# The first loads and the last three tiles of an adaptive feed-forward kernel, in another order

## What is computed

```python
q_emb = relu(cond @ W3 + b3)                              # 32 x 512
v = (64 * x + x.sum(axis=1, keepdims=True)) * q_emb[:, None, :]
h0 = relu(v @ W2 + b2)                                    # 2048 rows x 512
h = square(relu(h0 @ ternary(W_fc).T))                    # 2048 x 2048
hn = h * rsqrt(mean(h * h, axis=-1) + eps)
out = x + hn @ ternary(W_proj).T                          # 2048 x 512
```

## Time and profile before

| | us |
|---|---|
| median of 3 runs | 311.33 |
| lowest and highest of them | 311.01 and 311.59 |
| the profiled execution | 311.1 |
| its span, from the first to the last record | 309.3 |
| PE busy in it | 304.5 |
| ACT busy | 191.2 |
| DVE busy | 187.2 |
| POOL busy | 115.0 |

### The profile page before, as it was taken

One profiled execution on the slowest core, in us unless ns is written; L12 is line 12 of the kernel. 1 busy time (PEld: TensorE's weight loads), 2 busy tenths in 40 slices (PEclk: granted clock), 3 DMA queues, 4 the chain that ended last, 5 costly groups with the idle time before them and its releaser, 6 DMA issues.

```text
span 309.3 us, 3792 instructions
## 1 busy us (share of the span) xinstructions
PE 304.5 (98%) x1279; PEld 232.6 (75%) x1279; DVE 187.2 (61%) x311; ACT 191.2 (62%) x282; POOL 115.0 (37%) x106
## 2 busy tenths in 40 slices
PE   8999999999999999999999999999999999999995
PEld 8654545447888888888888888888888888888883
DVE  0689999994888778886257335942223484222245
ACT  1773566796999599976746444455554445555540
POOL 1044676646433323335333331353333314333330
PEclk9999999999999999999999999999999999999999
DMA  7993743362654044113005200340000034000003
GB/s 259 366 312 120 223 117 105 102 139 65 196 147 102 1 102 37 34 34 68 2 0 170 103 0 1 136 139 0 0 0 2 0 136 138 0 0 0 2 2 137
DMA packets 30293, 27.03 MB, mean 87 GB/s; under 512 B 17689, under 2 KB 19777, under 8 KB 30273
## 3 DMA queue, kind: packets, MB, share of 16 engines
q1 hardware_dynamic: 29936, 26.22, 29.3%
q10 hardware_dynamic: 336, 0.56, 0.5%
HBM read 18.39 MB, written 4.19 MB: 73 GB/s over the span
## 4 chain that ended last, share of the span: by engine, by line
PE 98%; DVE 0%; issue 0%; DVEq 0%
PE ps_out L382 38%; PE ps_acc L370 38%; PE ps_acc L354 18%; PE ps_out L341 2%; PE ps_out L332 1%; PE ps_acc L425 1%; PE ps_x L442 1%; PE ps_x L416 0%; DVE x_sb L587 0%; DVE x_t L517 0%; PE ps_x L422 0%; PE ps_acc L429 0%; PE ps_acc L437 0%; DVEq L504 0%
## 5 line engine op out<-in xcount | busy, mean ns | idle before, releaser
L265 POOL TENSOR_TENSOR wv_sb<-wv_sb 128x512 f32<-128x512 f32 x55 | 71.8, 1306 | 122.6 <-DVE y_lo L532 115.5
L370 PE MATMUL ps_acc<-h_hi,w_t 128*128 128x512 f32 x256 | 100.0, 391 | 0.0
L382 PE MATMUL ps_out<-w_t,y_hi 128*128 128x512 f32 x256 | 100.0, 391 | 0.0
L382 PE MATMUL ps_out<-w_t,y_lo 128*128 128x512 f32 x256 | 99.7, 389 | 0.0
L370 PE MATMUL ps_acc<-h_lo,w_t 128*128 128x512 f32 x256 | 99.6, 389 | 0.0
L530 DVE CAST y_hi<-x_t 128x512 fp32r<-128x512 f32 x64 | 32.6, 510 | 87.5 <-PE ps_out L382 73.0
L679 ACT ACTIVATE x_t<-ps_acc 128x512 f32<-128x512 f32 x64 | 37.9, 592 | 62.5 <-PE ps_acc L370 62.5
L354 PE MATMUL ps_acc<-x_t,wv_sb 128*128 128x512 f32 x128 | 56.3, 593 | 0.3 <-DVE x_t L517 0.3
L370 PEld LDWEIGHTS ps_acc<-h_lo,w_t 128*128 128x128 f32 x256 | 48.1, 188 | 10.2 <-issue 0.2
L370 PEld LDWEIGHTS ps_acc<-h_hi,w_t 128*128 128x128 f32 x256 | 48.0, 188 | 10.2 <-issue 0.2
L382 PEld LDWEIGHTS ps_out<-w_t,y_lo 128*128 128x128 f32 x256 | 48.1, 188 | 9.9
(11 more groups left out here) (60 smaller groups left out, 172.7 us busy)
## 6 DMA issues: line engine op xcount, KB each, us to landing
x_sb<-in_x_dram SPq DMA_DIRECT2D x5, 1024.0 KB, 5.4
raw<-in_L_ffn_W_fc_dram SPq DMA_DIRECT2D x8, 512.0 KB, 6.3
raw<-in_L_ffn_W_proj_dram SPq DMA_DIRECT2D x8, 512.0 KB, 4.2
out_dram<-x_sb SPq DMA_DIRECT2D x16, 256.0 KB, 2.1
x_odd<-in_x_dram SPq DMA_DIRECT2D x2, 1024.0 KB, 7.8
x_sb<-in_x_dram SPq DMA_DIRECT2D x4, 256.0 KB, 4.2
wv_sb<-in_L_cond_W_dram SPq DMA_DIRECT2D x4, 256.0 KB, 7.6
x_t<-in_L_cond_W_dram ACTq DMA_DIRECT2D x1, 512.0 KB, 4.7
```

Of the source, the lines that this page charges most:

```text
L265: engine.tensor_tensor(acc, acc, y_sq[:, v % SQ_RING, :], ALU.add).then_inc(sq_added, 1)
L370: last = pe.matmul(ps_acc[:, (UNITS + v) % ACC_RING, :], w_t[:, j, k * P:(k + 1) * P], part[:, k, g * BANK:(g + 1) * BANK], start=(k == 0 ...
L382: last = pe.matmul(ps_out[:, t, :], part[:, v % RING, t * P:(t + 1) * P], w, start=(opens(v) and part is y_hi), stop=(closes(v) and part i ...
```

## The change

Six edits go together.

1. The load of the query's weight moves from ACT's queue to SP's, right behind the four row tiles of x.
2. PE's first work becomes the sums of x: cond's turn, the biases' turn and the query's products leave their places. The turns stand behind row tile 2, the products behind row tile 3. One semaphore serves both turns, so cond's turned copy waits for the biases too.
3. Six matmuls on zeros stand at the start in place of seven.
4. The last three tiles (61, 62, 63) are projected row tile by row tile. sum_squares stands inside row tile 0, between tiles 62 and 63.
5. y_hi and y_lo of tiles 62 and 63 lie in the place of h0_hi and h0_lo of group 0, so their split waits for no projection. DVE adds tile 63's squares between the rounding and the remainder of tile 63, not ahead of tile 62.
6. The last output row tile is finished and written in two halves of 256 columns.

```diff
@@ constants
-WARM_UP = 7
+WARM_UP = 6
...
+    BY_ROWS = TILES - 3
+    SPARE = TILES - 2
...
+    def pieces(n):
+        whole = [(t, slice(0, BANK)) for t in range(TT)]
+        if n < GROUPS - 1:
+            return whole
+        return whole[:-1] + [(TT - 1, slice(0, BANK // 2)), (TT - 1, slice(BANK // 2, BANK))]
...
+        def y_part(whole, spare, v):
+            return whole[:, v % RING, :] if v < SPARE else spare[:, v - SPARE, 0:BANK]
+
+        def y_hi_of(v):
+            return y_part(y_hi, h0_hi, v)
+
+        def y_lo_of(v):
+            return y_part(y_lo, h0_lo, v)
@@ SP
             for t in range(TT):
                 sp.dma_start(x_sb[:, t, :], x_rows[0, :, t, :]).then_inc(x0_loaded[t], 16)
+            sp.dma_start(wq_sb[:], w_q.rearrange("(k p) d -> p k d", p=P)).then_inc(wq_loaded, 16)
             load_wv(0)
...
-                for t in range(TT):
+                for i, (t, cols) in enumerate(pieces(n)):
                     if n == 1:
-                        sp.wait_ge(merged, t + 1)
+                        sp.wait_ge(merged, i + 1)
                     else:
-                        sp.wait_ge(finished, TT * (n + 1) + t + 1)
-                    sp.dma_start(out_rows[STRETCHES[n + 1][0], t], x_res[:, t, :]).then_inc(stored, 16)
+                        sp.wait_ge(finished, TT * (n + 1) + i + 1)
+                    sp.dma_start(out_rows[STRETCHES[n + 1][0], t][:, cols], x_res[:, t, cols]).then_inc(stored, 16)
...
-            sp.wait_ge(stored, 16 * TT * GROUPS)
+            sp.wait_ge(stored, 16 * (TT * GROUPS + 1))
@@ PE
-            def project_last_two():
-
-                pe.wait_ge(split, TILES - 1)
-                project_tile(TILES - 2, 0)
-                project_tile(TILES - 2, 1)
-                pe.wait_ge(split, TILES)
-                project_tile(TILES - 1, 0)
-                project_tile(TILES - 1, 1)
-                for t in range(2, TT):
-                    project_tile(TILES - 2, t)
-                    project_tile(TILES - 1, t)
+            def project_by_rows():
+
+                for t in range(TT):
+                    for v in range(BY_ROWS, TILES):
+                        if t == 0:
+                            if v == TILES - 1:
+                                sum_squares(GROUPS)
+                            pe.wait_ge(split, v + 1)
+                        project_tile(v, t)
...
-            pe.wait_ge(ident_ready, 1)
-            pe.wait_ge(cond_loaded, 16)
-            for k in range(KQ):
-                last = pe.transpose(ps_acc[:, 0, k * BATCHES:(k + 1) * BATCHES], cond_sb[:, k * P:(k + 1) * P],
-                                    ident_f[0:BATCHES, 0:BATCHES])
-            last.then_inc(condt_done, 1)
             pe.wait_ge(consts_ready, 1)
             for t in range(TT):
-                if t == TT // 2:
-                    pe.wait_ge(condt_ready, 1)
-                    pe.wait_ge(biases_loaded, 32)
-                    pe.transpose(ps_acc[:, 0, KQ * BATCHES:KQ * BATCHES + 2 * KD], bias_sb,
-                                 ident_f[0:2 * KD, 0:2 * KD]).then_inc(biases_turned, 1)
-                    pe.wait_ge(wq_loaded, 16)
-                    for m in range(KD):
-                        for k in range(KQ):
-                            last = pe.matmul(ps_x[:, m * BATCHES:(m + 1) * BATCHES], wq_sb[:, k, m * P:(m + 1) * P],
-                                             cond_t[:, k, :], start=(k == 0), stop=(k == KQ - 1))
-                    last.then_inc(q_done, 1)
                 pe.wait_ge(x0_loaded[t], 16)
                 for k in range(KD):
                     last = sum_x_block(0, t, k)
                     if t == TT - 1:
                         last.then_inc(xt_done, 1)
+                if t == TT - 2:
+
+                    pe.wait_ge(ident_ready, 1)
+                    pe.wait_ge(cond_loaded, 16)
+                    for k in range(KQ):
+                        pe.transpose(ps_acc[:, 0, k * BATCHES:(k + 1) * BATCHES], cond_sb[:, k * P:(k + 1) * P],
+                                     ident_f[0:BATCHES, 0:BATCHES])
+                    pe.wait_ge(biases_loaded, 32)
+                    pe.transpose(ps_acc[:, 0, KQ * BATCHES:KQ * BATCHES + 2 * KD], bias_sb,
+                                 ident_f[0:2 * KD, 0:2 * KD]).then_inc(condt_done, 1)
+            pe.wait_ge(condt_ready, 1)
+            pe.wait_ge(wq_loaded, 16)
+            for m in range(KD):
+                for k in range(KQ):
+                    last = pe.matmul(ps_x[:, m * BATCHES:(m + 1) * BATCHES], wq_sb[:, k, m * P:(m + 1) * P],
+                                     cond_t[:, k, :], start=(k == 0), stop=(k == KQ - 1))
+            last.then_inc(q_done, 1)
...
             project(TILES - 4)
-            project(TILES - 3)
-            sum_squares(GROUPS)
-            project_last_two()
+            project_by_rows()
@@ DVE
             def split_y(v):
                 dve.wait_ge(y_ready, v + 1)
-                if v >= RING:
+                if RING <= v < SPARE:
                     dve.wait_ge(*projected_at(v - RING))
-                dve.tensor_copy(y_hi[:, v % RING, :], y[:, v % RING, :]).then_inc(hi_done, 1)
+                dve.tensor_copy(y_hi_of(v), y[:, v % RING, :]).then_inc(hi_done, 1)
+                if v == TILES - 1:
+                    add_squares(dve, v)
                 dve.wait_ge(hi_done, v + 1)
-                dve.tensor_tensor(y_lo[:, v % RING, :], y[:, v % RING, :], y_hi[:, v % RING, :], ALU.subtract).then_inc(split, 1)
+                dve.tensor_tensor(y_lo_of(v), y[:, v % RING, :], y_hi_of(v), ALU.subtract).then_inc(split, 1)
...
-                for t in range(TT):
+                for t, cols in pieces(r - 1):
                     dve.wait_ge(tile_summed, TT * r + t + 1)
-                    dve.scalar_tensor_tensor(out=x_res[:, t, :], in0=ps_out[:, t, :], scalar=rstd[:, t:t + 1],
-                                             in1=x_res[:, t, :], op0=ALU.mult, op1=ALU.add).then_inc(finished, 1)
+                    dve.scalar_tensor_tensor(out=x_res[:, t, cols], in0=ps_out[:, t, cols], scalar=rstd[:, t:t + 1],
+                                             in1=x_res[:, t, cols], op0=ALU.mult, op1=ALU.add).then_inc(finished, 1)
...
-            dve.wait_ge(biases_turned, 1)
...
-                if v == TILES - 2:
-                    add_squares(dve, TILES - 1)
                 split_y(v)
@@ ACT
             act.dma_start(cond_sb, cond).then_inc(cond_loaded, 16)
-            act.dma_start(wq_sb[:], w_q.rearrange("(k p) d -> p k d", p=P)).then_inc(wq_loaded, 16)
```

More of the change, by code:

```diff
@@ L188, in adaln_ffn @@
         biases_loaded = sem("biases_loaded")
-        biases_turned = sem("biases_turned")
         biases_ready = sem("biases_ready")
@@ L380, in project_tile @@
                     wait(pe, finished, TT * (r - 1) + t + 1)
-                for part in (y_hi, y_lo):
-                    last = pe.matmul(ps_out[:, t, :], part[:, v % RING, t * P:(t + 1) * P], w,
-                                     start=(opens(v) and part is y_hi), stop=(closes(v) and part is y_lo))
+                for part in (y_hi_of, y_lo_of):
+                    last = pe.matmul(ps_out[:, t, :], part(v)[:, t * P:(t + 1) * P], w,
+                                     start=(opens(v) and part is y_hi_of), stop=(closes(v) and part is y_lo_of))
                 if closes(v):
```

## The result

The changed kernel takes 313.17 us (median of 6 runs, 312.40 to 313.47), the kernel before 311.17 (median of 6, 310.69 to 311.59). The ratio is 1.0068, with a 95% interval of 1.0057 to 1.0079: slower by 2.0 us, clear of the 0.2% that a measurement can tell. The forecast was 311.9, no measurable change, with a range up to 312.7.

What follows compares the result with a forecast made beforehand. The prediction took PE to bound the kernel, with 304.5 of 309.3 us busy. Its terms, 0.73 + 0.44 + 0.10 - 0.75 = +0.52 us on 311.33, gave 311.9 us, range 310.9 to 312.7.

Steps and rivals of the forecast that it cites:

- the opening's sum: Opening: sums start 0.68 us earlier, but slow passes, turns and lost overlap make DVE's first product 0.73 us later.
- Slower, by the clock: Rival, opening: PE's clock rises later than 5.8 us, costing 0.47 per us; 312.8 us if 2 us later; chance 0.12.
- h0 starting before 11.6: Sign against the forecast, opening: h0's first pass was expected at 12.0 us in place of 11.31.
- the fixed rise: Opening: PE's clock was taken to rise from 1.2 to 2.4 GHz near 5.8 us, as in the profile before.
- The first pass of x: Opening: PE's sums of x start at 3.70 us instead of 4.38, once row tile 0 has landed.
- W3 landing: Opening: W3, behind x in SP's queue, lands near 7.4 us; PE asks near 8.7, a cover of 1.3 us.
- The handover: Opening: query's last pass to ACT's piece 0.39 us, piece 0.29, DVE 0.03 behind; DVE's product to h0 0.84.
- ACT's lateness: Behind the opening: h0's relus come some 1.1 us later, covered by 1.4 us at unit 5, so costing nothing.
- The standstill: End: PE waits 0.44 us ahead of sum_squares for DVE's addition, formerly covered by four passes.
- The halves: End: two half finishes on DVE take 0.84 us in sequence, 0.10 later than one whole.
- The last write: End: the half-size last write, further behind the others, gains 0.75 us; bounds 0.37 to 1.0.
- The end together: End: 0.44 standstill and 0.10 halves lost, 0.75 gained in the last write; bounds -0.9 to +0.3.

Runs made afterwards that it cites:

- a1_fill6: The changed kernel with six more matmuls on zeros on PE between the query's products and h0: 311.45 us, ratio 1.0015 to the kernel before.
- d1_wide_q: The changed kernel with the query's moving operand repeated from 32 to 128 columns: 311.42 us, ratio 1.0020 to the kernel before.
- c4_end_mid_whole: Opening of the kernel before, changed end with sum_squares two passes later and the last row tile whole: 310.33 us, ratio 0.9984.
- a3_opening: The changed opening (edits 1 to 3) with the end of the kernel before: 313.50 us, ratio 1.0084.
- c1_q_last: The kernel before with only the biases' turn and the query's products moved behind the last row tile's sums: 313.99 us, ratio 1.0101.
- b1_idle: The kernel before with one added wait: h0's first matmul waits for DVE's third product, not the first: 312.06 us, ratio 1.0035.
- a2_fill2: The changed kernel with two more matmuls on zeros between the query's products and h0: 312.51 us, ratio 1.0047 to the kernel before.
- c2_idle_q: The kernel before in its own order, with one added wait on PE behind the query's products: 313.31 us, ratio 1.0070.
- a4_end: The changed end (edits 4 to 6) with the opening of the kernel before: 310.78 us, ratio 0.9994.
- c3_end_mid: Opening of the kernel before, changed end with sum_squares two passes later on PE, halves kept: 310.13 us, ratio 0.9977.
- b3_end_late: Opening of the kernel before, changed end with sum_squares four passes later on PE, ahead of tile 63: 310.51 us, ratio 0.9989.
- b2_halves: The kernel before with edit 6 alone, the last row tile finished and written in two halves: 311.06 us, ratio 1.0008.

## Why the prediction was wrong

**The step that failed** is the opening's sum. It counted the stretch between the query's last pass and h0 as time and nothing else ("DVE's first product starts at ... 11.2 ... 0.73 us later"). I had in hand that PE would do nothing between the last of the query's products and h0, and that those passes are small, and put this stretch's effect on the clock at nothing, without a reason. The runs show 3.41 us at a granted clock of 0.50 behind it, which cost 1.7 us: with fillers (a1_fill6) or wide passes (d1_wide_q) they are gone. The opening's measured +2.6 lies outside my bounds for it, -0.2 to +1.5.

**The rival that came true in name only.** "Slower, by the clock" had 0.12. Its mechanism was a later rise, from a gap ahead of the sums. In the profile after, the rise came earlier instead. The trace's record of the full clock begins at 5.82 us in the kernel before and at 4.31 after, and between 3.65 and 6.56 over the 15 profiles, one of each kernel. The clock then fell again, behind the idle stretch, which no rival named. The Trainium skill, page "TensorE: Matmul & The Clock Gate", section on the clock gate, says that the moment of the rise varies from run to run. The traces agree, with the 2.9 us between 3.65 and 6.56, as far as single profiles of nearly the same opening can show it. The same page, in its section on oscillation, tells of waits between bursts of matmuls that bring the clock down; I had used the page for the rise alone. Its waits are of some 3 to 5 us, though. Here 1.26 us behind narrow passes was enough, and the measurement decides.

**A sign that came true by luck.** I had said that h0 starting before 11.6 would show me wrong. It started at 11.20, and not at my 12.0, mainly because the rise came 1.5 us earlier, worth 0.7 by the prediction's own 0.47 per us. In d1_wide_q, with the rise at 5.4, it starts at 11.85. So the order of this opening was costed well, and the fixed rise was one draw of several.

**What was right, term by term:**
- The first pass of x at 3.70: 3.64.
- W3 landing near 7.4: 2.65 + 4.9 = 7.5.
- The pace on zeros: 0.224 said, an average that takes in a first step of 0.35. The other steps are 0.213, as on x. It changes nothing.
- The handover: ACT 0.37 us behind the query's last pass (0.39 said), 0.30 long (0.29), DVE's product to h0 0.83 (0.84).
- The opening without the clock: 0.73 said. d1_wide_q stands 0.63 above the kernel before and the end gives 0.2 back, so the opening costs about 0.8.
- ACT's lateness costs nothing: the first relu of h0 at 18.31 (18.13 before), with no wait of PE for it.
- The standstill: 0.44 said, 0.47 in the weight loads. But not all of it is new time on PE. From the last pass ahead of sum_squares to PE's last pass it is 5.77 us and was 4.58; four more passes in between are 0.91 of that, so the net cost is about 0.3.
- The halves: 0.84 said, 0.88 measured.
- The last write: 1.75 said, 1.8 measured. I had put 0.5 of the gain down to the distance between the writes, which c4_end_mid_whole bears out, and 0.37 to the halved bytes, of which 0.2 shows, and 0.05 net of the later issue.
- The end together: -0.21 said, -0.2 measured, [-0.5, +0.1] by its interval. By the profiles the standstill costs 0.3 and the stretch behind PE gains 0.53 (3.29 to 2.76), where 0.44 and 0.65 stood in the sum: part of the hit is two errors that cancel.

So with the clock kept up (a1_fill6, d1_wide_q) the change is +0.5 to +0.6 us, near the 0.52 of the sum. The low clock adds 1.7.

## What to carry to other kernels

An idle stretch of PE costs its length. By what stands right ahead of it, it can also cost a stretch of low clock behind it: here half of 3.41 us, in one profile half of 6.83. Look at the granted clock behind every wait that a reordering puts behind small matmuls. If the wait can't be covered by real work, cover it with matmuls on zeros, or widen the small ones where that costs no time. And the last write gained more here from its distance to the one ahead than from being small.

## What the runs showed of the hardware

- The clock fell behind 1.26 us of idle time with 16 float32 passes of 32 columns right ahead of it (all 14 runs of the changed kernel, a3_opening and c1_q_last), and didn't behind 1.26 and 1.43 us with passes of 128 columns ahead (d1_wide_q and b1_idle: none of 16 runs). A shorter idle stretch (a2_fill2, 0.73 us: four of seven) and one in the middle of the opening (c2_idle_q, 1.9 us: two of four) are in between.
- The low stretch was 3.41 us long in three profiles (after, c1_q_last, c2_idle_q) and 6.83 in one (a3_opening).
- A float32 pass of 32 columns and one of 128 have the same distance, 0.112 us at the full clock.
- A write of 256 KB to memory took 2.0 us with nothing right ahead of it and 2.4 to 2.5 as the last of four that are issued 0.7 to 0.9 us apart. The last half, 128 KB, took 1.8 where the first half was issued 1.1 us behind the whole write ahead (after, a4_end, c3_end_mid), and 2.1 to 2.2 where it was 0.8 to 0.9 (b3_end_late, b2_halves).
